# Feed-forward convolution on a product that stays in PSUM, with three bank pairs

## What is computed

```python
def bit_linear(x, w):                 # act_quant: 127 / max|x| per token; weight_quant: ternary
    return jnp.einsum('bsd,hd->bsh', act_quant(x), weight_quant(w))
h = bit_linear(x, w1)                                        # (4, 1024, 2048)
h = depthwise_conv1d(h.transpose(0, 2, 1), conv_w, conv_b)   # three taps over the tokens
h = jax.nn.silu(h.transpose(0, 2, 1))
return bit_linear(h, w2)                                     # (4, 1024, 512)
x = x + jnp.tanh(g_ffn[0]) * ffn(_layernorm(x))
```

## Time and profile before

| | us |
|---|---|
| median of 3 executions | 1868.02 (1867.94 to 1870.0) |
| the profiled execution, its own time | 1868.89 |
| its span in the profile | 1867.1 |
| DVE busy in the span | 1204.4 (65%) |
| PE busy in the span | 1669.6 (89%) |
| ACT, POOL busy in the span | 827.8, 719.0 |

### The profile page before, as it was taken

The page is one execution under the profiler, slowest core; times in us unless marked ns, Lnnn a source line. Parts: engine busy times, 40 slices in busy tenths (PEclk is TensorE's granted clock), DMA queues, the critical chain, the costliest instruction groups (busy, mean ns, idle before and its releaser), DMA issues. The chain is left out here.

```text
span 1867.1 us, 23800 instructions
## 1 busy us (share of the span) xinstructions
PE 1669.6 (89%) x8754; PEld 1026.6 (55%) x8754; DVE 1204.4 (65%) x2205; ACT 827.8 (44%) x866; POOL 719.0 (39%) x314
## 2 busy tenths in 40 slices
PE   6888899999999999999999999999986876877758
PEld 5666678888886544454445444544453433444434
DVE  6777645443345667657865786667359478399793
ACT  2111222222220344424562456345647767677666
POOL 1131000000000488856875687567825043151340
PEclk9999999999999999999999999999999897998989
DMA  6656456544434411202231213221331020200201
GB/s 238 238 186 213 168 193 223 176 160 152 157 130 158 148 58 67 98 20 103 98 106 48 102 59 113 69 103 36 128 136 53 23 90 23 89 2 1 91 0 46
DMA packets 107811, 200.81 MB, mean 108 GB/s; under 512 B 7616, under 2 KB 33216, under 8 KB 107712
## 3 DMA queue, kind: packets, MB, share of 16 engines
q1 hardware_dynamic: 107712, 199.49, 30.4%
HBM read 124.75 MB, written 74.71 MB: 107 GB/s over the span
## 5 line engine op out<-in xcount | busy, mean ns | idle before, releaser
L726 POOL TENSOR_TENSOR acc<-acc,pr 128x1024 f32<-128x1024 f32 x188 | 448.3, 2385 | 134.4 <-ACT pr L756 117.8
L756 ACT ACTIVATE pr<-ps,mcol 128x1024 f32<-128x1024 f32 x256 | 284.4, 1115 | 366.5 <-PE ps L1452 363.9
L1014 DVE CUSTOM_DVE_ANT_0 junk<-ps,mbias 128x512 bf16<-128x512 f32 x512 | 333.1, 688 | 129.3 <-PE ps L1427 125.2
L1464 PE MATMUL ps<-pr,vv 128*64 128x512 f32 x1024 | 274.7, 618 | 0.0
L731 POOL TENSOR_TENSOR h_first<-h_first,last_tap 128x1024 f32<-128x1024 f32 x44 | 104.8, 2386 | 274.0 <-ACT last_tap L897 274.0
L707 POOL MEMSET nmt<- 128x128 f32 x1 | 0.2, 204 | 364.2 <-DVE chl L1227 364.2
L1427 PE MATMUL ps<-kh,qh 64*128 64x512 f32 x512 | 123.0, 452 | 13.1 <-DVE nmv L1014 12.0
L1533 PE MATMUL ps<-xiT,w1q 128*128 128x512 bf16 x512 | 123.8, 389 | 5.0 <-ACT xiT L746 5.0
L726 POOL TENSOR_TENSOR acc<-pr 128x1024 f32<-128x1024 f32 x32 | 76.8, 2401 | 122.0 <-ACT pr L756 122.0
L1427 PEld LDWEIGHTS ps<-kh,qh 64*128 64x128 f32 x512 | 51.0, 185 | 130.9 <-issue 99.3
L1690 PE MATMUL ps<-w2q,hq 128*128 128x512 bf16 x512 | 121.2, 390 | 1.5 <-ACT hq L925 0.8
(11 more groups left out here) (173 smaller groups left out, 3218.8 us busy)
## 6 DMA issues: line engine op xcount, KB each, us to landing
craw<-in_ctxT SPq DMA_DIRECT2D x8, 2048.0 KB, 9.6
xa<-in_x SPq DMA_DIRECT2D x8, 1024.0 KB, 6.2
wraw<-in_w1T SPq DMA_DIRECT2D x16, 512.0 KB, 7.6
wraw<-in_w2T SPq DMA_DIRECT2D x16, 512.0 KB, 8.1
q_split<-kqh SPq DMA_DIRECT2D x32, 256.0 KB, 2.0
q_split<-kql SPq DMA_DIRECT2D x32, 256.0 KB, 2.3
base<-lna SPq DMA_DIRECT2D x8, 1024.0 KB, 9.1
k_split<-kqh SPq DMA_DIRECT2D x32, 256.0 KB, 2.1
```

The source lines that it names most:

```text
L726: nc.gpsimd.tensor_tensor(acc[:, blk % 2, :], first, pr[:, (8 * blk + j) % NP, :], ALU.add).then_inc(pool_acc, 1)
L756: act.activation(pr[:, u % NP, :], ps[:, 2 * (u % 2):2 * (u % 2) + 2, :].rearrange("p a t -> p (a t)"), ACT.Exp, bias=mcol[:, (u // 64) * ...
L1014: dve.tensor_tensor_reduce(out=(junk1 if n < LEAD and n % 2 else junk)[:, e, :], in0=ps[:, first_bank(n) + e, :], in1=mbias[:, b % 2, kk * ...
L1464: last = pe.matmul(ps[64 * e:64 * e + 64, 6 + blk % 2, :], vv[g % 2][:, j, 64 * e:64 * e + 64], pr[:, u % NP, e * CH:(e + 1) * CH], start= ...
```

## The change

The scaled product is no longer copied to SBUF. g(j) writes it back in place, in PSUM, and c1, c2 and c0 read it there. The product's pairs are now three, in banks 0 to 5 (`pair(j)`), so the transposes have one pair left, banks 6 and 7. The steps at the edge leave out the missing column (1023 columns in c2, c0 and p) in place of reading a zero column. The order of the two additions is turned round: c0(j) now waits for c2(j), and p(j) waits for c2(j) and c0(j); T(j) waits for p(j). F(j) waits for c0(j-3) and c2(j-3) where it waited for g(j-2). T(j) waits for silu(j-1) where it waited for silu(j-2). In batch 0, F(2) now uses banks 4 and 5 and waits until DVE has taken the last product of the attention.

```diff
-        gp = sb("gp", [P, 3, S + 2], F32)
+        def pair(j):
+            return ps[:, 2 * (j % 3):2 * (j % 3) + 2, :].rearrange("p a t -> p (a t)")
@@ POOL
                     pool.wait_ge(act_d, b * D_ACT_N + D_ACT[f"c2_{j}"])
-                    nc.gpsimd.tensor_tensor(h[j % 3], h[j % 3], last_tap[j % 2][:], ALU.add).then_inc(pool_tap, 1)
+                    pool.sem_inc(pool_tick, 1)
+                    pool.wait_ge(dve_d, b * D_DVE_N + D_DVE[f"c0{j}"])
+                    nc.gpsimd.tensor_tensor(h[j % 3][:, 0:S - 1], h[j % 3][:, 0:S - 1], last_tap[j % 2][:, 0:S - 1], ALU.add).then_inc(pool_tap, 1)
@@ ACT
-                    act.activation(h[j % 3], gp[:, j % 3, 1:S + 1], ACT.Identity, bias=convb[:, j:j + 1],
+                    act.activation(h[j % 3], pair(j), ACT.Identity, bias=convb[:, j:j + 1],
                                    scale=convw[:, j, 1:2]).then_inc(act_d, 1)
                     if j >= 2:
                         act.wait_ge(pool_tap, b * KH + j - 1)
-                    act.activation(last_tap[j % 2][:], gp[:, j % 3, 2:S + 2], ACT.Copy, scale=convw[:, j, 2:3]).then_inc(act_d, 1)
+                    act.activation(last_tap[j % 2][:, 0:S - 1], pair(j)[:, 1:S], ACT.Copy, scale=convw[:, j, 2:3]).then_inc(act_d, 1)
...
-                    act.activation(hT[:, :, j * P:(j + 1) * P], ps[:, 4 + 2 * (j % 2):6 + 2 * (j % 2), :].rearrange("p a (i t) -> p (a i) t", t=P),
+                    act.activation(hT[:, :, j * P:(j + 1) * P], ps[:, 6:8, :].rearrange("p a (i t) -> p (a i) t", t=P),
@@ DVE
-            if j >= 3:
-                dve.wait_ge(dve_d, b * D_DVE_N + D_DVE[f"c0{j - 3}"])
-            dve.tensor_tensor(gp[:, j % 3, 1:S + 1], ps[:, 2 * (j % 2):2 * (j % 2) + 2, :].rearrange("p a t -> p (a t)"),
-                              row[:], ALU.mult).then_inc(dve_d, 1)
+            dve.tensor_tensor(pair(j), pair(j), row[:], ALU.mult).then_inc(dve_d, 1)
...
                 for j in range(KH):
-                    if j + 2 < KH:
-                        dve_scaled(dve, b, j + 2)
-                    dve.wait_ge(pool_tap, b * KH + j + 1)
-                    dve.scalar_tensor_tensor(out=h[j % 3], in0=gp[:, j % 3, 0:S], scalar=convw[:, j, 0:1], in1=h[j % 3],
+                    done(f"g{j}")
+                    dve.wait_ge(act_d, an + D_ACT[f"c2_{j}"])
+                    dve.scalar_tensor_tensor(out=h[j % 3][:, 1:S], in0=pair(j)[:, 0:S - 1], scalar=convw[:, j, 0:1], in1=h[j % 3][:, 1:S],
                                              op0=ALU.mult, op1=ALU.add).then_inc(dve_d, 1)
                     if j >= 2:
                         biggest(j - 2)
+                    if j + 2 < KH:
+                        dve_scaled(dve, b, j + 2)
@@ PE
-            if j >= 2:
-                pe.wait_ge(dve_d, b * D_DVE_N + D_DVE[f"g{j - 2}"])
+            if j >= 3:
+                pe.wait_ge(dve_d, b * D_DVE_N + D_DVE[f"c0{j - 3}"])
+                pe.wait_ge(act_d, b * D_ACT_N + D_ACT[f"c2_{j - 3}"])
...
                 for j in range(3):
+                    if b == 0 and j == 2:
+                        pe.wait_ge(dve_free5, use5["y", B - 1, NT - 1] + 1)
                     if b or j == 2:
                         pe_first(pe, b, j)
-                if b == 0:
-                    pe.wait_ge(dve_free5, use5["y", B - 1, NT - 1] + 1)
                 for j in range(KH):
                     if j + 3 < KH:
                         pe_first(pe, b, j + 3)
-                    pe.wait_ge(dve_d, dn + D_DVE[f"c0{j}"])
-                    if j >= 2:
-                        pe.wait_ge(act_d, an + D_ACT[f"silu{j - 2}"])
+                    pe.wait_ge(pool_tap, b * KH + j + 1)
+                    if j >= 1:
+                        pe.wait_ge(act_d, an + D_ACT[f"silu{j - 1}"])
```

More of the change, by code:

```diff
@@ L312, in flamingo_gated_block @@
         dve_tick = sem("dve_tick")
+        pool_tick = sem("pool_tick")
         dve_ln = sem("dve_ln")
@@ L416, in flamingo_gated_block @@
         D_DVE, D_DVE_N = counts(["g0", "g1"]
-                                + [f"{w}{j + 2 * (w == 'g') - 2 * (w == 'hmax')}" for j in range(KH) for w in ("g", "c0", "hmax")
+                                + [f"{w}{j + 2 * (w == 'g') - 2 * (w == 'hmax')}" for j in range(KH) for w in ("c0", "hmax", "g")
                                    if not (w == "g" and j + 2 >= KH) and not (w == "hmax" and j < 2)]
@@ L1124, in c_dve @@
                 finish(B - 1, i)
-            for i in range(3):
-                dve.memset(gp[:, i, 0:1], 0.0)
-                dve.memset(gp[:, i, S + 1:S + 2], 0.0)
             dve.wait_ge(act_ln, LN_ACT["row"])
@@ L1528, in pe_first @@
         def pe_first(pe, b, j):
-            if j >= 2:
-                pe.wait_ge(dve_d, b * D_DVE_N + D_DVE[f"g{j - 2}"])
+            if j >= 3:
+                pe.wait_ge(dve_d, b * D_DVE_N + D_DVE[f"c0{j - 3}"])
+                pe.wait_ge(act_d, b * D_ACT_N + D_ACT[f"c2_{j - 3}"])
             for t in range(2):
                 for k in range(KD):
-                    last = pe.matmul(ps[:, 2 * (j % 2) + t, :], w1q[:, k, j * P:(j + 1) * P], xiT[:, k, t * 512:(t + 1) * 512],
+                    last = pe.matmul(ps[:, 2 * (j % 3) + t, :], w1q[:, k, j * P:(j + 1) * P], xiT[:, k, t * 512:(t + 1) * 512],
                                      start=k == 0, stop=k == KD - 1)
@@ L1670, in ffn @@
                         pe_first(pe, b, j + 3)
-                    pe.wait_ge(dve_d, dn + D_DVE[f"c0{j}"])
-                    if j >= 2:
-                        pe.wait_ge(act_d, an + D_ACT[f"silu{j - 2}"])
+                    pe.wait_ge(pool_tap, b * KH + j + 1)
+                    if j >= 1:
+                        pe.wait_ge(act_d, an + D_ACT[f"silu{j - 1}"])
                     for i in range(NT):
-                        last = pe.transpose(ps[:, 4 + 2 * (j % 2) + i // 4, (i % 4) * P:(i % 4 + 1) * P], h[j % 3][:, i * P:(i + 1) * P], ident[:])
+                        last = pe.transpose(ps[:, 6 + i // 4, (i % 4) * P:(i % 4 + 1) * P], h[j % 3][:, i * P:(i + 1) * P], ident[:])
                     last.then_inc(pe_ct, 1)
```

## The result

The changed kernel takes 1824.76 us in the median of 4 executions (1822.27 to 1827.91), the kernel before beside it 1867.98 (1863.62 to 1870.0): a ratio of 0.9773 with a 95% interval of 0.9749 to 0.9796, thus 43 us less. The profiled execution took 1822.27 us, its span is 1820.5.

A forecast was written before the change was run, and what follows sets the result against it. DVE was taken to bound the hidden part; 11.3 + 11.3 + 11.05 us less in batches 1 to 3 and 7.4 in batch 0 make 41, the span falling from 1867.1 to 1826, forecast 1828, range 1820 to 1845.

The forecast's parts named there:

- The bound and the hold: Hidden part: DVE bounds the turn; c0, reading two SBUF inputs, is held until 1.08 us behind GpSimd's p.
- Writing to PSUM: Rival, 10%: g reading and writing the same PSUM bank takes 2.26 us, making the kernel slower at 1886.
- The turn: DVE's steady turn in the hidden part: 1.13 + 1.13 + 1.20 = 3.46 us in place of 4.045.
- The margin at T: Steady turn on PE: T(j+1) waits for p(j+1) at 7.13 and silu(j) at 6.84, 0.3 us to spare.
- the layout: All engines' steady turns laid out from c0(j)'s start; F(j+3) may start at 1.31, needed at 9.25 by g(j+3).
- The sum: Hidden parts: 11.3 us less in batches 1 and 2, 11.05 in batch 3, 7.4 in batch 0, together 41.
- the opening: Batches 1 to 3, start of the hidden part: c0(3) at 12.97 us behind g(0), with a 1.28 us table load.
- The end: Last turns of a hidden part: T(15) waits for silu(14), the single pair; last hmax ends at 62.1 us.
- PE's clock: Rival, 9%: PE falls to half clock in the opening, losing 3.5 us a batch: 1842; full clock was expected.
- the rival that GpSimd still holds c0: Rival, 6%: c0 stretched 0.05 us a steady turn and 2 us a batch in the opening: 1839.

The follow-up runs named there:

- short addition: The kernel before with GpSimd's addition p on 8 of its 1024 columns, a measurement only: 1811.0 us, ratio 0.970.
- the run with DVE's additions: Changed kernel with T(15) in banks 4 and 5 and p(14), p(15) on DVE in place of GpSimd: 1820.12 us, ratio 0.9752 against the kernel before.

## Why the prediction was right

**The bound and the hold.** The reading of the earlier trace rows held: c0 with one input in PSUM has one length, 1.275 us (predicted 1.266), with p beside it or not; the c0 at 1496.64 above lies wholly inside the two additions that begin at 1495.67 and takes 1.28. The short addition on the kernel before shows that with GpSimd out of the way c0 is never long.

**Writing to PSUM.** g was put at 1.21 with 2.26 as the upper bound; it takes 1.224. That rival, the only one that made the kernel slower than before, is out by its own row. The rule of the Trainium skill that I weighed (VectorE: DVE Perf Modes, section The TRN2 errata, more cycles for PSUM) is again not seen in c0: 1.275 us for 1023 columns from PSUM and, with the short addition, 1.276 for 1024 from SBUF.

**The turn.** Predicted 3.46, measured 3.45, without idle time on DVE. The margin at T held too: in the steady turns of batch 1 T waits for p, never for silu. One reading of the layout was wrong without harm. The prediction has F(j+3) needed at 9.25 us behind c0(j)'s start, but g(j+3) comes one turn behind g(j+2), at 2.33 + 3.46 = 5.8: c0(5) of batch 1 starts at 1509.63, F(8) at 1510.97 and g(8) at 1515.40. F then has some 2.5 us to spare and not 6, and with one pair fewer, where it is needed a turn sooner, none.

**The sum.** Predicted 41 us, measured 42.9 in the hidden parts. Batch 0 (7.4 predicted and measured) and batch 3 (11.05 and 10.95) are right. Batches 1 and 2 are mis-sized: 11.3 predicted, 12.3 measured each. The term is the opening, where I counted the table load of the earlier trace rows in every batch. ACT loads a table ahead of silu(0) in batches 0 and 3 alone, before and after the change. Without it silu(0) follows c2(2) at once (1498.06 + 1.11 to 1499.22), and c0(3) starts 12.0 us behind g(0), where batch 3 needs 13.1 (predicted 12.97). The end fell out as written, T(15) behind silu(14). The prediction's remark that what the turns don't bring "is from the opening" is too simple: the opening brings more (8.3 us in batch 1) and the longer end takes 3.15 back. Both are in its laid-out times, though the remark does not say so. Of the 3.2 us by which the whole time lies under the predicted 1828, 2 come from this term and the rest is not told apart from the start of the hidden part, which moves by more than that.

**PE's clock.** Predicted at full in the opening, and so it was: behind a gap of 1.57 us ahead of F(3), F(3) takes 1.90 us and T(0) 1.10, both at a granted clock of 1.00 (2.4 GHz). Before, a gap of 4.35 us in the same batch was followed by T(0) at 0.50 (1.2 GHz), 1.97 us. In the end T(14) and T(15) stand behind gaps of 2.36 and 1.20 us and run at 0.50, 1.97 and 1.94 us. The gap right ahead does not decide it alone: T(13) stands behind one of 2.35 us (1540.97) and still takes 1.09 at 1.00, while in the run with DVE's additions T(13), behind 2.34 us, takes 1.97 at 0.50. Why the two differ stays open.

**The order's share.** I wrote, under the rival that GpSimd still holds c0, that the turned order alone brings most of the gain, 1839. It brought 1835.5. By the rival's own times the hold costs a steady turn 3.67 + 1.08 - 4.73 = 0.02 us, not the 0.05 that it states; measured it is 0.07 or 0.08. What the prediction did not say is the other side: the PSUM operand without that order is a loss of 11 us, and operand and order with two pairs are one of 17. The gain isn't a sum of three parts; the order makes the product's long stay in PSUM affordable, and the third pair does the same.

## What to carry to other kernels

When GpSimd and DVE share a stage, look at the spread of each DVE instruction (min, median, max) and at where its inputs lie. Two long instructions that shut each other out cost each other nothing where the order keeps them apart in time, and turning round two additions may be nearly enough, as it was here. Keeping a tile in PSUM for its readers prolongs the life of its banks: count the time from the write to the last reader against the number of pairs before you take the copy away. At both ends of a pipelined stage another chain sets the time than in its middle, so an edit worth nothing in the steady turn may pay there, and the other way round.

## What the hardware showed beyond expectation

The hold looks like a shutting out and not like a slowing: a c0 that starts inside p ends 1.08 us behind p's end, whether it had started 0.27 us or 1.38 us before it (with the order alone: 1514.97 to 1516.32 with p to 1515.24, and 1499.76 to 1502.22 with p from 1498.79 to 1501.14). That is about the 1.05 us that the prediction works out for 1024 columns, so it does nearly all of them after p. The addition is shut out by c0 in turn (3.34 us above). A multiplication that reads one tensor from PSUM and one from SBUF and writes back into the same PSUM banks takes 14 ns more than the one that writes to SBUF, and ACT reads the same banks 30 ns faster than SBUF.
